# A transformer decoder layer with routed experts: the expert-tile loop with its first turn inside, a later scatter of the second list, and three token lists in place of four

## The reference

```
x = LN(x + self_attention(x))            # 8 heads, blocks of 64 tokens, biases
x = LN(x + cross_attention(x, ctx))      # 16 heads
logits = x @ Wr.T                        # 8 experts
probs  = softmax(logits); the two highest are kept and renormalised to sum 1
h      = silu(x @ W1[e].T)               # 128 -> 512, for each kept expert e
x = LN(x + sum over the two experts of weight[e] * (h @ W2[e].T))
```

## Time and profile before

| what | us |
|---|---|
| median of three runs | 1382.2 |
| the profiled execution | 1379.32 |
| its span in the profile | 1377.4 |
| PE busy in the span | 962.4 |
| POOL busy in the span | 445.7 |
| scatter DMAs on POOL, 128 | 123.8 busy, first at 800.3, last at 961.8 |
| gather DMAs on POOL, 128 | 129.9 busy |
| granted PE clock, mean | 0.858 of full speed |

### The profile page before, as it was taken

One profiled execution on the slowest core, in us unless ns is written; L12 is line 12 of the kernel. 1 busy time (PEld: TensorE's weight loads), 2 busy tenths in 40 slices (PEclk: granted clock), 3 DMA queues, 4 the chain that ended last, 5 costly groups with the idle time before them and its releaser, 6 DMA issues.

```text
span 1377.4 us, 30644 instructions
## 1 busy us (share of the span) xinstructions
PE 962.4 (70%) x10082; PEld 815.0 (59%) x10083; DVE 857.2 (62%) x2598; ACT 729.5 (53%) x1364; POOL 445.7 (32%) x535
## 2 busy tenths in 40 slices
PE   4888888884999999999997402111698977676740
PEld 2777777773888888888886301000587866555530
DVE  3688888885788888888885730000454666566552
ACT  3666766653776767767763300000575765555531
POOL 3123333332010010010102357777002055654555
PEclk8989998887999999999997555555799999899985
DMA  6930000000001000000000002111233334443431
GB/s 193 290 87 15 15 15 15 15 9 18 13 11 21 10 11 17 10 19 10 0 1 1 1 38 71 51 59 52 55 93 86 92 95 106 99 107 99 101 87 53
DMA packets 157233, 73.72 MB, mean 54 GB/s; under 512 B 76034, under 2 KB 151042, under 8 KB 157188
## 3 DMA queue, kind: packets, MB, share of 16 engines
q1 hardware_dynamic: 148996, 56.34, 15.6%
q0 software_dynamic: 8192, 16.79, 4.2%
HBM read 22.76 MB, written 37.75 MB: 44 GB/s over the span
## 4 chain that ended last, share of the span: by engine, by line
PE 38%; DVE 22%; issue 21%; ACT 13%; another core or an unknown queue 2%; POOL 2%; DMA 1%; DVEq 1%; ACTq 0%; SPq 0%; POOLq 0%
PE bank L449 9%; PE bank L451 8%; PE bank L450 8%; PE bank L551 4%; DVE at L925 4%; DVE X L1002 3%; ACT XTa L746 3%; DVE mx L909 3%; ACT qzh L746 3%; PE bank L537 3%; PE bank L528 2%; DVE st L992 2%; ACT vz_self L755 1%; DVE z L937 1%
## 5 line engine op out<-in xcount | busy, mean ns | idle before, releaser
L424 POOL DMA_INDIRECT wst<-yd,pos x128 | 129.9, 1015 | 222.2 <-DVE z L1117 105.6
L449 PE MATMUL bank<-XTa,qzh 128*128 128x128 f16 x768 | 146.0, 226 | 37.7 <-ACT XTa L746 37.7
L925 DVE TENSOR_TENSOR at<-bank,rc 64x32 f32<-64x32 f32 (+1 forms) x768 | 153.5, 200 | 14.4
L831 ACT ACTIVATE pr<-bank 128x512 f32<-128x512 f32 x96 | 57.3, 597 | 192.4 <-remote 106.5
L760 ACT ACTIVATE pr<-bank 128x512 f32<-128x512 f32 x192 | 114.1, 594 | 79.5 <-PE bank L528 78.3
L909 DVE TENSOR_REDUCE mx<-bank 128x8 bf16<-128x512 f32 x192 | 132.9, 692 | 28.7 <-PE bank L451 23.1
L451 PE MATMUL bank<-XTa,qzl 128*128 128x128 f16 x768 | 146.5, 226 | 0.0
L450 PE MATMUL bank<-XTa,qzh 128*128 128x128 f16 x768 | 146.3, 226 | 0.0
L764 ACT ACTIVATE pt<-bank 128x512 f32<-128x512 f32 x192 | 113.3, 590 | 60.5 <-PE bank L537 60.1
L411 POOL DMA_INDIRECT xd<-XTa,pos x128 | 123.8, 968 | 65.3 <-issue 65.3
L1098 DVE TENSOR_TENSOR xtl<-xs,xth 128x512 f16<-128x512 f32 x96 | 66.4, 695 | 120.4 <-ACT xth L832 71.5
(11 more groups left out here) (202 smaller groups left out, 3084.5 us busy)
## 6 DMA issues: line engine op xcount, KB each, us to landing
yd<-at SPq DMA_DIRECT2D x96, 128.0 KB
xd<-blank SPq DMA_DIRECT2D x2, 3072.0 KB, 20.7
X<-x_dram SPq DMA_DIRECT2D x16, 256.0 KB, 2.8
wst<-w_dram SPq DMA_DIRECT2D x16, 256.0 KB, 2.7
xd<-blank SPq DMA_DIRECT2D x1, 4096.0 KB, 28.3
cin<-ctx_in_dram SPq DMA_DIRECT2D x16, 256.0 KB, 2.8
out_dram<-z SPq DMA_DIRECT2D x16, 256.0 KB
xd<-blank SPq DMA_DIRECT2D x1, 2048.0 KB, 21.5
```

Of the source, the lines that this page charges most:

```text
L424: nc.gpsimd.indirect_dma_start(out=yg[k][:, t, :], out_offset=None, in_=yd[chunk_of(n)], in_offset=bass.IndirectOffsetOnAxis(ap=pos[k][:, ...
L449: nc.tensor.matmul(out_, lh, rh, start=start, stop=False, **kw)
L831: nc.scalar.activation(s32[n % 4][:], bank[n % 4][:], ACT.Silu, scale=IWS)
L925: m = nc.vector.tensor_tensor(dst, src, r, ALU.mult)
```

## The change

Three things are done. The list boundaries become 0 to 16, 16 to 48, 48 to 64 (4, 8 and 4 groups): 24, 40 and 24 row tiles, together 88, or 22 turns; `FJ` becomes 13, so turns 13 to 21 finish 9 groups and 7 stand behind the loop. On PE turn 0 moves into the hardware loop; for that, `f_ev` starts at 2, by one POOL memset, so that the wait of `down` is the same in every turn, and SP's wait counts two more. And POOL waits for `f_h` to reach 10 (five row tiles through `up`) before it scatters list two.

```diff
-CHUNKS = ((0, 16), (16, 40), (40, 56), (56, 64))
+CHUNKS = ((0, 16), (16, 48), (48, 64))
@@ SP, store
-                wait_apart(sp, f_ev, n + CB[c] + 1, ld_w, 96)
+                wait_apart(sp, f_ev, n + CB[c] + 3, ld_w, 96)
@@ POOL
+            nc.gpsimd.memset(z2[:, 1, 0:1], 0.0).then_inc(f_ev, 2)
@@ POOL, scatter
             for n, (t0, t1) in enumerate(SEGS):
+                if t0 == CHUNKS[1][0]:
+                    pool.wait_ge(f_h, 10)
                 if n >= 2:
                     pool.wait_ge(sent[n - 2], 32 * (SEGS[n - 2][1] - SEGS[n - 2][0]))
@@ PE, down
-                if c == 0 and not (isinstance(i, int) and i < 2):
-                    pe.wait_ge(f_ev, i - 1)
+                if c == 0:
+                    pe.wait_ge(f_ev, i + 1)
@@ PE, tile loop
-            four(0, word, False)
-            with pe.Fori(1, NJ - 1) as j:
-                word = carried()
-                four(j, word, False)
+            pe.reg_mov(experts, word)
+            with pe.Fori(0, NJ - 1) as j:
+                four(j, carried(), False)
             four(NJ - 1, carried(), True)
```

## The result

The changed kernel takes 1385.78 us (median of 20 runs, 1382.42 to 1393.11), the kernel before 1382.09 (20 runs). The ratio is 1.0035, 95% interval 1.0020 to 1.0049: slower by 0.2 to 0.5%, inside what I had called no change. In a later session it was 1.0031 (1.0012 to 1.0050). The profiled execution took 1385.53 us with a span of 1383.7.

What follows compares the result with a forecast made beforehand. It took PE's completions, signalled late while POOL emits indirect DMAs, as the bound. Terms 0 + 6 - 0.4 = +5.6 us gave an execution of 1384.9; with the median 2.9 us over the profiled execution, 1388, range 1368 to 1401.

Steps and rivals of the forecast that it cites:

- What bounds the kernel: Expert part, turn 0: PE's completions are signalled late while POOL emits indirect DMAs; 119 us lost.
- the crawl: PE's slow stretch beside POOL's scatter in turn 0: 54 matmuls in 123.4 us before the change.
- Turn 0 inside the loop: PE's first turn moved into the hardware loop: 0 us, between -1 and +1.
- The hold: POOL's scatter of list two held back until f_h 10: +6 us, ends -14 and +10.
- 4.3 us of freedom: PE is slowed only 4.3 us after POOL's held scatter starts at 859.8, at 864.1.
- the drain of 13.0: PE stays slowed 13.0 us after the last held scatter DMA, as behind the run of 119 DMAs.
- the run of eight: POOL's eight gather DMAs in turn 6, with a drain of 1.6 us; using that drain gave -4.4 us.
- The three lists: Two turns fewer, four more groups finished behind the loop: 22.9 - 72.5 + 49.2 = -0.4 us.
- rival two: Groups behind the loop cost 14.4 us, not 12.3, POOL being the bound: about 1398 us; chance 0.16.
- part one: Turn 0 inside the loop: 0 us, between -1 and +1 for register moves and f_ev waits.
- One (new code crawls): Turn 0's instructions arrive slowly beside the scatter; the loop removes the crawl, 97 us less: 1285; chance 0.15.
- Three (a mild crawl): Short drain or higher rate in warm code, the hold -4 to -14 us: 1368 to 1378; chance 0.16.

Runs made afterwards that it cites:

- hold26: The changed kernel with POOL's wait at f_h 26 in place of 10; 1390.82 us, one run, slowed session.
- paced kernels: Kernel before with other list boundaries and later scatter DMAs issued in pairs tied to row tiles; 1307.46 us (0.9478) and, denser, 1300.75 us (0.9413), slowed sessions.
- scatter_first_b: Kernel before with no row tile loaded until all four lists are scattered; 1381.63 us, ratio 1.0015, slowed session.
- hold_only: Kernel before with only the wait for f_h 10 ahead of list two's scatter; 1242.32 us, ratio 1.0112, free session.
- lists_only_b: Kernel before with only the three lists of 4, 8 and 4 groups; 1380.49 us, ratio 0.9967, slowed session.

## Why the prediction was right, step by step

**What bounds the kernel: right in the slowed condition, which is the one that the profile before and the result belong to, and incomplete.** Two parts of the reading were tested in the slowed condition. That the crawl comes with POOL's DMAs back to back beside PE held in hold26, in the paced kernels and in scatter_first_b; that it is not new code held in hold26. The third part, one path for PE's completions that is slow, is argued from the late rows of ACT and DVE: no run isolates it, nor the rival that recording the run slows PE, since every run is recorded. The earlier trace rows names q8 alone; the same view has three packets of a second instruction queue, q14, which changes nothing in the argument. That PE was slowed at all is a condition of the session. The profile before could not show this, and the prediction took it for a property of the kernel. Had the result been taken in a free session, the parts measured there (+14 to +16 and +23 to +24 us alone) point to a clearly slower kernel. That case was not among the rivals: where the prediction supposes that the scatter costs PE nothing, it puts the hold at 0, and leaves out that PE then waits for list two's rows (11.4 us in hold_only).

**Turn 0 inside the loop: forecast 0, within 1 us.** Measured only in the free session, +0.24% (0.01 to 0.47). That is 3 us, 0.1 to 5.8; a little more than I gave it. What costs it was not looked into.

**The hold: forecast +6 us, -14 to +10.** By the timed ratio +6.6. Step by step: POOL was to start 14.5 us behind PE (859.8 less 845.3) and did (855.4 less 840.9); 4.3 us of freedom were 5.1; about 57 matmuls in 130.6 us were 65 in 130.4; the drain of 13.0 was 13.5. Taking the drain from the row of the long run rather than from the run of eight (1.6) was the choice that decided the sign. Twelve us of work let through first do not pay for moving 122 us of scatter by as much.

**The three lists: forecast -0.4 us; whether they gain anything is not shown.** The ratio of lists_only_b gives -4.6 (0.8 to 8.3 less), the medians of the same session +0.7. Its one profile has 536.5 us from PE's first W1 matmul to the end, where before has 532.1 (1377.4 less 845.3). In the changed kernel the intervals came out near what was taken: eight from group 0 to group 8, 143.7 us (forecast 140.4); from group 8 to group 15, 90.85 against 43.3 from group 12 to group 15 before, which is +47.6 (forecast +49.2). The six plain ones behind the loop have a mean of 12.3, (90.85 - 16.8)/6, and the one at the new list is 16.8 where 18.7 was taken. So rival two's 14.4 was wrong: that mean held the interval at the list boundary. Nothing in the intervals makes a gain of 4.6 us; if there is one, the prediction has no term for it, and where it comes from stays open.

**The sum.** By the ratios 6.6 - 4.6 and up to 3 of part one make 2 to 5 us; measured 4.8 (2.8 to 6.8). The forecast of 1388, +5.6 us, was 2 us above the median. In part this is luck: if the ratios of the parts hold, the term of the lists was 4 us too high and that of part one up to 3 us too low (measured in a free session only), and the two errors cancel in part.

**Rivals.** One (new code crawls): out, by the changed kernel itself and by hold26. Two: out, as above. Three (a mild crawl): out in this condition.

## What to carry to other kernels

Count what runs beside what, then check how fast it runs: 120 us of overlap were worth next to nothing in one condition and everything in the other. Where a long run of DMAs from the general-purpose engine's queue slows an engine, moving the run changes little; breaking it into pairs with gaps, tied to that engine's progress, gave 5 to 6% in the slowed condition. And when work is cut at one end, look at who takes over: 8 row tiles less (23 us) gave 8 us at best and perhaps nothing, since four groups went from beside a turn (5.6 us each) to behind it (12.3).

## What the runs showed of the hardware that was not expected

The same kernel took 1380 us in two sessions and 1226 to 1228 in two others, apart by far more than nearly all of its runs within a condition (1374 to 1391 and 1221 to 1233 us). In the slowed ones, PE's completions reach other engines up to 87 us late while POOL emits DMAs back to back (22 to 87 in the profile before, 8 to 84 in that of the changed kernel). PE falls from 12.7 matmuls per us to between 0.4 and 0.5, mostly in steps of 2.80 us, and goes on so for 13 us after the last DMA. It has 50 to 60 matmuls of grace first, and pairs of DMAs with gaps of 1 to 3 us leave it at 11.5 per us. All runs here are recorded by the profiler; whether the recording has a part in it could not be tried.
